# A perceiver block on one core: xn formed by GpSimd, z by column halves, and the dispatch sums and later logit transposes placed behind the first gate matmuls

## The reference, cut to what matters

```python
x = x + xattn(layernorm(x), ctx)          # 128 queries, 12544 context rows
x = x + gated_long_conv(layernorm(x))     # two stages, by DFT matrices
z = layernorm(x)                          # outer norm of the third step
# the third step, soft mixture of E=16 experts with S=64 slots each:
xn = layernorm(z) * norm_g + norm_b
se = (layernorm(slot_embeds) * slot_g + slot_b) * scale
logits = einsum('bnd,esd->bnes', xn, se)             # 128 tokens x 1024 slots
dispatch = softmax(logits, over the 128 tokens)
combine = softmax(logits, over the 1024 slots)
slots = einsum('bnd,bnes->besd', xn, dispatch)
gate = gelu(slots @ Wg + bg); up = slots @ Wu + bu   # 256 -> 512 per expert
eout = (gate * up) @ Wd + bd                         # 512 -> 256
x = x + einsum('bns,bso->bno', combine, eout)
```

## Time and profile before

| | us |
|---|---|
| median of 3 executions | 195.43 |
| lowest, highest | 195.1, 199.83 |
| the profiled execution: its time | 195.87 |
| its span, first to last instruction | 193.8 |
| PE busy | 187.5 |
| DVE busy | 124.4 |
| ACT busy | 109.3 |
| POOL busy | 82.3 |

### The profile page before, as it was taken

How to read it: one execution, slowest core, us unless ns; L and a number is a source line. 1 busy time by engine, 2 the same in 40 slices (tenths; PEclk the granted TensorE clock), 3 DMA queues, 4 the chain that set the end, 5 groups by cost and what they waited for, 6 DMA issues and landing times.

```text
span 193.8 us, 3919 instructions
## 1 busy us (share of the span) xinstructions
PE 187.5 (97%) x1244; PEld 144.9 (75%) x1244; DVE 124.4 (64%) x269; ACT 109.3 (56%) x225; POOL 82.3 (42%) x61
## 2 busy tenths in 40 slices
PE   7999999999999999999999999999999999999993
PEld 4887999999999999999999989974544544454451
DVE  2377997788778779877778778753673523524431
ACT  1568877687677777777775542967358421122210
POOL 2249999876778876877878013100000000000000
PEclk9999999999999999999999999999999999999999
DMA  5998977875784786884595399999999999973100
GB/s 158 292 358 259 317 245 234 268 248 178 252 229 131 270 265 190 278 249 148 167 230 118 71 382 380 354 373 368 380 365 382 276 368 274 269 196 108 44 0 27
DMA packets 24908, 47.01 MB, mean 243 GB/s; under 512 B 1601, under 2 KB 11969, under 8 KB 24897
## 3 DMA queue, kind: packets, MB, share of 16 engines
q1 hardware_dynamic: 23664, 43.52, 70.4%
q10 hardware_dynamic: 1232, 3.35, 7.0%
HBM read 46.73 MB, written 0.13 MB: 242 GB/s over the span
## 4 chain that ended last, share of the span: by engine, by line
PE 87%; DMA 7%; ACT 2%; SPq 1%; DVE 0%; issue 0%; ACTq 0%
PE bank L663 15%; PE bank L416 10%; PE bank L677 7%; PE bank L457 6%; PE bank L461 6%; PE bank L459 6%; PE bank L429 5%; PE bank L433 5%; PE bank L431 5%; DMA raw<-in_ctx_dram 5%; PE bank L442 5%; PE bank L687 2%; PE bank L550 2%; PE bank L694 2%; PE bank L569 2%; DMA W_sb<-in_L_xattn_W_dram 2%
## 5 line engine op out<-in xcount | busy, mean ns | idle before, releaser
L955 POOL TENSOR_TENSOR c_lo<-raw,c_hi 128x1024 fp32r<-128x1024 f32 (+1 forms) x25 | 53.9, 2157 | 21.6 <-ACT c_hi L781 21.1
L1038 DVE TENSOR_TENSOR cT_lo<-bank,cT_hi 128x512 fp32r<-128x512 f32 (+1 forms) x50 | 31.7, 675 | 10.1 <-ACT cT_hi L773 8.8
L773 ACT ACTIVATE cT_hi<-bank 128x512 fp32r<-128x512 f32 (+1 forms) x48 | 25.6, 586 | 9.3 <-PE bank L416 9.3
L457 PE MATMUL bank<-c_hi,pT_hi 128*128 128x258 f32 x98 | 30.0, 306 | 0.0
L461 PE MATMUL bank<-c_hi,pT_lo 128*128 128x258 f32 x98 | 27.7, 283 | 0.0
L459 PE MATMUL bank<-c_lo,pT_hi 128*128 128x256 f32 x98 | 27.6, 281 | 0.0
L950 POOL TENSOR_TENSOR c_hi<-raw,zero 128x512 fp32r<-128x512 f32 (+1 forms) x25 | 25.6, 1025 | 1.9 <-DMA raw<-in_ctx_dram 1.9
L416 PE MATMUL bank<-tab,raw 128*128 128x128 f32 x196 | 25.6, 273 | 0.1
L788 ACT ACTIVATE pT_hi<-bank 128x512 fp32r<-128x512 f32 (+1 forms) x25 | 14.8, 590 | 15.0 <-PE bank L442 14.9
L416 PEld LDWEIGHTS bank<-tab,raw 128*128 128x128 f32 x196 | 22.1, 142 | 0.5 <-DMA raw<-in_ctx_dram 0.3
L429 PE MATMUL bank<-cT_hi,q_hi 128*128 128x512 f32 (+1 forms) x50 | 21.5, 430 | 0.3 <-DVE q_lo L1087 0.3
(11 more groups left out here) (172 smaller groups left out, 299.7 us busy)
## 6 DMA issues: line engine op xcount, KB each, us to landing
raw<-in_ctx_dram SPq DMA_DIRECT2D x24, 512.0 KB, 3.9
bias<-biases_dram ACTq DMA_DIRECT2D x10, 320.0 KB, 7.0
late_gu<-in_L_ffn_Wg_dram SPq DMA_DIRECT2D x3, 1024.0 KB, 10.7
late_gu<-in_L_ffn_Wu_dram SPq DMA_DIRECT2D x3, 1024.0 KB, 11.2
late_d<-in_L_ffn_Wd_dram SPq DMA_DIRECT2D x3, 1024.0 KB, 13.8
early_gu<-in_L_ffn_Wg_dram SPq DMA_DIRECT2D x4, 512.0 KB, 4.6
early_gu<-in_L_ffn_Wu_dram SPq DMA_DIRECT2D x4, 512.0 KB, 5.3
early_d<-in_L_ffn_Wd_dram SPq DMA_DIRECT2D x4, 512.0 KB, 5.0
```

What stands on the lines that cost most here:

```text
L457: nc.tensor.matmul(bank[6 + r][:, 0:D + 2], ph, c_hi[:, slot, t, :], start=(t == 0), stop=False)
L773: nc.scalar.activation(cT_hi[:, g % 2, h, 0:n], bank[h][:, 0:n], ACT.Copy).then_inc(cThi_rdy, 1)
L955: nc.gpsimd.tensor_tensor(c_lo[:, slot, 0:nt, :], raw[:, slot, 0:nt, :], c_hi[:, slot, 0:nt, 0:D].bitcast(fp32), ALU.subtract).then_inc(cl ...
L1038: nc.vector.tensor_tensor(cT_lo[:, g % 2, h, 0:n], bank[h][:, 0:n], cT_hi[:, g % 2, h, 0:n].bitcast(fp32), ALU.subtract).then_inc(cTlo_rdy, 1)
```

## The change

It does four things.

1. POOL forms `xn` (two instructions, multiply and add, 128x256) in place of DVE.
2. DVE makes z in two column halves, each with an increment of `z_rdy`; PE transposes each half as it comes, each with an increment of `zT_ps`. ACT now makes `xnT[:, 0]`, DVE `xnT[:, 1]`.
3. The logits of piece 1 are computed as 256 columns (pairs 1 and 2) around the shift and 128 columns (pair 3) behind them.
4. `dispatch_sums` and `transpose_logits(1)` go from in front of the first gate matmuls to behind them, ahead of the logits of piece 2.

```diff
--- before.py
+++ after.py
@@ -183,7 +183,7 @@
         stat_rdy = sem("stat_rdy")
         se_rdy, seT_ps, seT_rdy = sem("se_rdy"), sem("seT_ps"), sem("seT_rdy")
         gs_rdy = sem("gs_rdy")
-        shift_rdy = sem("shift_rdy")
+        shift_rdy, xg_rdy = sem("shift_rdy"), sem("xg_rdy")
         spec_ps, spec_rdy = sem("spec_ps"), sem("spec_rdy")
         cT_ps, cThi_rdy, cTlo_rdy = sem("cT_ps"), sem("cThi_rdy"), sem("cTlo_rdy")
@@ -555,21 +555,18 @@
             keep_busy(6)
-            pe.wait_ge(z_rdy, 1)
             for k in range(DK):
-                last = nc.tensor.transpose(bank[(7, 1)[k]][:, k * P:(k + 1) * P], xh[:, k * P:(k + 1) * P], ident)
-            last.then_inc(zT_ps, 1)
+                pe.wait_ge(z_rdy, k + 1)
+                nc.tensor.transpose(bank[(7, 1)[k]][:, k * P:(k + 1) * P], xh[:, k * P:(k + 1) * P], ident
+                                    ).then_inc(zT_ps, 1)
             keep_busy(4)
             pe.wait_ge(xnT_rdy, DK)
             pe.wait_ge(seT_rdy, 4)
-            def logits(n, chunks=range(DK)):
-                lo, hi = PIECES[n]
-                for k in chunks:
-                    last = nc.tensor.matmul(bank[L_BANK[n]][:, 0:(hi - lo) * P], xnT[:, k, :],
-                                            seT[:, k, lo * P:hi * P], start=(k == 0), stop=(k == DK - 1))
-                if k == DK - 1:
-                    last.then_inc(L_ps, 1)
+            def logits(n, lo, hi, k):
+                at = PIECES[n][0]
+                return nc.tensor.matmul(bank[L_BANK[n]][:, (lo - at) * P:(hi - at) * P], xnT[:, k, :],
+                                        seT[:, k, lo * P:hi * P], start=(k == 0), stop=(k == DK - 1))
             def transposed_logits():
@@ -643,12 +640,12 @@
             transposed_logits()
             first_logits()
-            logits(1, (0,))
+            logits(1, 1, 3, 0)
             shift_logits()
-            logits(1, (1,))
+            logits(1, 1, 3, 1)
+            logits(1, 3, 4, 0)
+            logits(1, 3, 4, 1).then_inc(L_ps, 1)
             gather(0)
-            dispatch_sums()
-            transpose_logits(1)
@@ -704,7 +701,10 @@
                         pe.wait_ge(gate_rdy, p - 1)
                     hidden_of(p, 0, (6, 7)[p % 2], gate_ps)
                 if p == 0:
-                    logits(2)
+                    dispatch_sums()
+                    transpose_logits(1)
+                    logits(2, 4, PAIRS, 0)
+                    logits(2, 4, PAIRS, 1).then_inc(L_ps, 1)
                     first_logits_back()
                     transpose_dispatch(1)
@@ -845,9 +845,8 @@
                                      ).then_inc(seT_rdy, 1)
             act.wait_ge(zT_ps, 1)
-            k = 1
-            nc.scalar.activation(xnT[:, k, :], bank[1][:, k * P:(k + 1) * P], ACT.Identity,
-                                 scale=col[:, 3, k:k + 1], bias=col[:, 4, k:k + 1]).then_inc(xnT_rdy, 1)
+            nc.scalar.activation(xnT[:, 0, :], bank[7][:, 0:P], ACT.Identity,
+                                 scale=col[:, 3, 0:1], bias=col[:, 4, 0:1]).then_inc(xnT_rdy, 1)
             act.wait_ge(xn_rdy, 1)
             nc.scalar.activation(xn_hi[:, :], xn[:, :], ACT.Copy).then_inc(xnhi_rdy, 1)
@@ -965,6 +964,12 @@
             power(1, rstd[:, 0:1], mv[:, 1:2], 1)
             power(2, se_rstd[:, :], se_mv[:, :, 1], PAIRS)
             power(3, rstd[:, 0:1], mv[:, 1:2], 1)
+
+            pool.wait_ge(ld_row, 32)
+            pool.wait_ge(z_rdy, 2)
+            nc.gpsimd.tensor_tensor(xn[:, :], xh[:, :], g_row[:, 0, :], ALU.mult).then_inc(xg_rdy, 1)
+            pool.wait_ge(xg_rdy, 1)
+            nc.gpsimd.tensor_tensor(xn[:, :], xn[:, :], g_row[:, 1, :], ALU.add).then_inc(xn_rdy, 1)
         @block.vector
@@ -1161,15 +1166,12 @@
             nc.vector.tensor_scalar(mv[:, 1:2], mv[:, 1:2], 1.0 + EPS, EPS * EPS, ALU.mult, ALU.add
                                     ).then_inc(var_rdy, 1)
             dve.wait_ge(rstd_rdy, 4)
-            nc.vector.tensor_scalar(xh[:, :], x2[:, :], mv[:, 0:1], rstd[:, 0:1], ALU.subtract, ALU.mult
-                                    ).then_inc(z_rdy, 1)
-            dve.wait_ge(ld_row, 32)
-            dve.wait_ge(z_rdy, 1)
-            dve.wait_ge(zT_ps, 1)
-            nc.vector.tensor_scalar(xnT[:, 0, :], bank[7][:, 0:P], col[:, 3, 0:1], col[:, 4, 0:1],
+            for h in range(2):
+                nc.vector.tensor_scalar(xh[:, cols(h)], x2[:, cols(h)], mv[:, 0:1], rstd[:, 0:1],
+                                        ALU.subtract, ALU.mult).then_inc(z_rdy, 1)
+            dve.wait_ge(zT_ps, 2)
+            nc.vector.tensor_scalar(xnT[:, 1, :], bank[1][:, P:2 * P], col[:, 3, 1:2], col[:, 4, 1:2],
                                     ALU.mult, ALU.add).then_inc(xnT_rdy, 1)
-            link(nc.vector.tensor_tensor(xn[:, :], xh[:, :], g_row[:, 0, :], ALU.mult))
-            nc.vector.tensor_tensor(xn[:, :], xn[:, :], g_row[:, 1, :], ALU.add).then_inc(xn_rdy, 1)
             def dispatch_max(n):
                 lo, hi = PIECES[n]
```

## The result

The changed kernel takes 197.52 us, the median of 10 executions (197.05 to 198.1), against 195.48 (194.88 to 199.83) for the kernel before. The ratio is 1.0095 with a 95% interval of 1.008 to 1.011: about 1.9 us slower. The ratio leaves out slow executions, such as the one of 199.83 us. 197.1 was forecast, in a range of 195.7 to 198.3.

What follows compares the result with a forecast made beforehand. PE was taken as the bound (busy 47.15 of 47.40 us from the second gate); gather(1) 1.70 us later made 195.87 into 197.57, less 0.44 to the runs' median: 197.1 forecast, range 195.7 to 198.3.

Steps and rivals of the forecast that it cites:

- z by halves and the start of the logits: Ahead of the logits: ACT's seT sets their start at 127.50 as before; gain 0, bounds 0.1 earlier to 0.25 later.
- xn on POOL: Beside the logits: two POOL instructions of 0.65 us each, xn ready about 128.0, hidden because gather(0) wants it at 130.0.
- Rival 2: Ahead of gather(0): POOL takes 1.65 us per xn instruction, the first gather starts 0.9 later, total 198.0; chance 0.10.
- Piece 1 as 256 and 128 columns: Logits ahead of gather(0): the split stalls PE at the shift for 0 to 0.1 us, cost taken as 0.05.
- The first gate: First gate matmuls: start at 131.04 instead of 131.24, 0.20 us earlier, with PE idle for half a microsecond there.
- The chain: From comb's transposes through DVE and ACT to gather(1): starts 2.26 us later, takes 6.00, so gather(1) comes 1.70 later.
- The end: Behind gather(1): PE is busy without a break to 187 us, so nothing of the 1.70 us delay is given back.
- Rival 1: At gather(1): chain takes 4.7 us or less, PE's own work decides, gather(1) about 0.4 later, total 195.7; chance 0.12.
- Rival 3: Around the first gate: PE's pauses drop its clock to 1.2 GHz, costing about another 6 us, total 203; chance 0.04.
- the last sign that was named: Behind 139 us: the forecast would also be wrong if PE waits for a weight load there; no size given.

Runs made afterwards that it cites:

- e3: The kernel before with only xn moved from DVE to POOL; ratio to the kernel before 0.9999 (0.9984 to 1.0015).
- e1: The changed kernel with dispatch_sums and transpose_logits(1) put back in front of the first gate; ratio to the kernel before 0.9994 (0.9977 to 1.0011).
- e2: The kernel before with only dispatch_sums and transpose_logits(1) moved behind the first gate; ratio to the kernel before 1.0067, run again 1.0106.
- e4: The changed kernel with ACT's logits copies and disp_hi ahead of gate 0's table load and GELU; ratio to the kernel before 1.0034 (1.001 to 1.0058).

## Why the prediction was right

**z by halves and the start of the logits.** The reading that ACT's four `seT` instructions and not z set the start held. The second half of z ended at 126.36, 0.96 us ahead of the logits (forecast: 126.5 and 127.5, 1.0), and the logits didn't start earlier for it (3.19 us behind the first `seT` against 3.18). Cost 0, as said.

**xn on POOL.** 0.73 and 0.72 us instead of 0.65 each, ready 0.72 behind the start of the logits instead of 0.5, hidden all the same: the change and e3 agree. Rival 2 is out; `disp` at 129.33 waits for PE alone.

**Piece 1 as 256 and 128 columns.** Forecast 0.05, measured 0.16 to 0.18 (e1 against before, the change against e2). The step was undersized around the shift: from 128.32 the first 256 columns took 0.51 to the shift and the shift 0.30 to the next, where 0.43 and 0.22 were reckoned. For the same reason `disp` came only 0.06 earlier than before (2.01 behind the logits against 2.07), not 0.2; nothing waited for it.

**The first gate.** Forecast 0.20 earlier, measured 0.08 in the change and 0.26 in e2, which has no split (forecast without its 0.05: 0.25). The mechanism was right, ACT's copy of the slots as the releaser; the difference is the split above.

**The chain.** Forecast that the transposes would come 2.26 later; it was 2.51, by the split (0.12 more) and by the sum (0.24 from its start to that of the transposes, where I took 0.12 out of bounds of 0.12 to 0.30). Forecast 6.00 from there to gather(1); measured 5.84. 0.13 of that was hidden in the trace of before, as ACT's rows of before and of the change show:

```profile
135.13 0.60 ACT L864 ACTIVATE comb<-bank 128x512 f32<-128x512 f32 x1
137.32 0.58 ACT L863 ACTIVATE comb<-bank 128x512 f32<-128x512 f32 x1
```

GELU to this copy took 0.66 before (from 134.47) and takes 0.53 now (from 136.79). Before, the copy started 0.05 behind the end of PE's logits of piece 2 (133.10 + 1.98), which it reads; the rows name no releaser, so that it waited for them is my reading. The two errors have opposite signs: gather(1) came 1.79 later, forecast 1.70. That the sum came so near is in part luck. The wait of 1.06 us, forecast as "some 1.3", is smaller because PE itself arrived later by the split, the sum and the pause before the exponentials.

**The end.** Nothing was to be given back; 0.10 was: the delay is 1.79 at gather(1), 1.69 at the second gate, 1.7 at the span's end (68.0 - 66.3). The kernel before had waited for `hid` in that stretch: DVE's `hid` ended at 138.92 (138.23 + 0.69) and its transposes started at 138.98, while in the change it ended at 140.26 and they started at 140.54. The ratio gives 1.86 us on 195.48. The two profiles of the same changed kernel differ by 0.3 us behind the second gate (68.0 and 68.3 with 13.75 in both), so what lies between 1.7 and 1.86 can't be told apart. Of the 0.42 us between the forecast of 197.1 and the median of 197.52, 0.09 is gather(1)'s; the rest lies within the scatter that was allowed for (197.05 to 198.1 for the changed kernel).

**Rivals.** Rival 1 needed a chain of 4.7 us or less; e4 made such a chain, and gather(1) then started at PE's pace, 4.77 us behind the transposes against the 4.55 to 4.75 worked out: there `disp_lo` ended 4.10 us behind the transposes. It also showed rival 1's time to have been too low: 0.72 instead of 0.4 later, for the split and the sum. Rival 3: the granted clock stayed at 1.00 across both pauses, the upper level. Nor did PE wait for a weight load behind 139 us, the last sign that was named.

## What to carry to other kernels

Work that is moved behind something else costs nothing only as long as the chain it starts has that much to spare; read the slack as the time between the end of the chain's last link and the moment its consumer gets there, less the hand-over (here 0.56 us), and set it against the delay (here 2.5 us). Work that stood beside a wait frees less than its own length when it is moved away: what was moved had taken 0.78 us ahead of the gate, and at most 0.26 was gained. Nor is all of that time work: 0.22 of it was idle. An engine's queue may hold a table load or another stage's instruction in the middle of such a chain; taking that out of it (e4) gave back more than half of the loss.

## What the runs showed of the hardware

The table load for GELU took 1.28 us in the change and in e4, as in the earlier trace rows, and GELU started 0.01 us behind it (135.50, 136.79); the load itself started 0.02 us behind the last exponential's accumulator. The Trainium skill, ScalarE: Activation LUTs, under What ACT_TABLE_LOAD costs, gives about 1283 ns for the load, which the rows meet, and a further 1380 ns of drain at every switch, which no row here shows; the measurement decides.

PE stood still for 0.37 us ahead of the first gate and for 1.0 us ahead of gather(1) without a fall of its granted clock (1.00 in every window up to 188.5 us). In the last stretch of the changed kernel's profile the mean is lower, and the second window shows where:

```profile
188.50:195.30 6.80, 3.33 (x23) 1.63 (x21) 0.91 (x2) 0.60 (x1) 0.00 (x0) 0.95 0.06 19
194.50:195.30 0.80, 0.00 (x0) 0.00 (x0) 0.00 (x0) 0.00 (x0) 0.00 (x0) 0.54 0.00 0
```

It fell only in the last 0.8 us of the span; PE's last matmul had ended at 192.61 (191.91 + 0.70), and the windows from there to 194.5 have 1.00. So it slowed no matmul: from the last down matmuls to the last mix it took 2.48 us (189.43 to 191.91), as in the kernel before (187.95 to 190.43). The second profile of the same kernel has 0.99 in its last stretch.

The shift's two records of 128 columns take 0.22 us to the next start in the kernel before (129.15 to 129.37), but 0.29 to 0.30 in the four profiles with the split (128.83 to 129.13 in the change), where PE gets to it just as `diag` is ready. What adds the 0.08 wasn't tried.
